# First-layer heads around the change of batch: GpSimd and the loads in the loop's order, and the batch-0 sums placed beside the row maxima

## What is computed

```python
q = jnp.einsum('bpd,hde->bphe', resid_pre, W_Q) + b_Q    # k, v alike
q = _apply_rotary(q, cos, sin)                           # k alike
scores = jnp.einsum('bqhd,bkhd->bhqk', q, k) / ATTN_SCALE
scores = jnp.where(causal[None, None], scores, 0)
max_v = jnp.max(jnp.abs(scores), axis=-1, keepdims=True)
sgn = jnp.sign(scores)
attn_w = sgn * jnp.exp(sgn * scores - max_v)
attn = attn_w / (jnp.sum(jnp.abs(attn_w), axis=-1, keepdims=True) + 1e-06)
z = jnp.einsum('bkhd,bhqk->bqhd', v, attn)
out = jnp.einsum('bqhd,hdm->bqm', z, W_O) + b_O
x = x + out
```

## Time and profile before

| | us |
|---|---|
| median of three executions | 864.09 |
| lowest and highest | 862.94, 867.29 |
| the profiled execution | 865.04 |
| its span, first to last instruction | 863.3 |
| TensorE busy | 828.1 |
| VectorE busy | 646.3 |
| ScalarE busy | 525.3 |
| GpSimd busy | 465.8 |
| mean granted share of TensorE's clock | 0.994 |

### The profile page before, as it was taken

One profiled execution on the slowest core, in us unless ns is written; L12 is line 12 of the kernel. 1 busy time (PEld: TensorE's weight loads), 2 busy tenths in 40 slices (PEclk: granted clock), 3 DMA queues, 4 the chain that ended last, 5 costly groups with the idle time before them and its releaser, 6 DMA issues.

```text
span 863.3 us, 14805 instructions
## 1 busy us (share of the span) xinstructions
PE 828.1 (96%) x4549; PEld 627.4 (73%) x4549; DVE 646.3 (75%) x1350; ACT 525.3 (61%) x1106; POOL 465.8 (54%) x399
## 2 busy tenths in 40 slices
PE   8899999999989999989998999999999999999997
PEld 6678788777878888766887887764444447888886
DVE  5898888999998888998376865868788634676553
ACT  3778788787867888863644533336576554454442
POOL 4565555666665556551666776623300426656774
PEclk9999999999999999999999999999999989999999
DMA  4222222322422223122665357412441132334442
GB/s 157 93 98 87 98 97 97 106 81 87 152 74 99 98 97 110 61 69 60 208 210 182 131 163 275 138 57 73 137 136 51 57 99 93 123 123 142 152 162 65
DMA packets 57426, 99.20 MB, mean 115 GB/s; under 512 B 8272, under 2 KB 19024, under 8 KB 57360
## 3 DMA queue, kind: packets, MB, share of 16 engines
q1 hardware_dynamic: 57360, 98.39, 34.3%
HBM read 71.88 MB, written 9.57 MB: 94 GB/s over the span
## 4 chain that ended last, share of the span: by engine, by line
PE 64%; issue 10%; POOL 10%; DVE 10%; ACT 4%; DMA 2%; SPq 0%; DVEq 0%; POOLq 0%; ACTq 0%
PE ps L974 10%; PE ps L951 10%; PE ps L960 9%; PE ps L319 6%; PE ps L382 5%; PE ps L330 4%; POOL q_sin L526 3%; PE ps L343 3%; PE ps L370 3%; PE ps L1642 2%; PE ps L1523 2%; PE ps L357 2%; PE ps L1612 2%; POOL wqk_lo L513 2%; DVE nm L1834 2%
## 5 line engine op out<-in xcount | busy, mean ns | idle before, releaser
L1098 POOL TENSOR_TENSOR ew_lo<-ew_raw,ew_hi 128x768 fp32r<-128x768 f32 x68 | 128.6, 1892 | 56.7 <-ACT ew_hi L1064 48.5
L1050 ACT ACTIVATE hid_hi<-guw 128x512 fp32r<-128x512 f32 x68 | 43.0, 632 | 156.2 <-POOL guw L1114 106.2
L1153 DVE TENSOR_TENSOR hid_lo<-guw,hid_hi 128x512 fp32r<-128x512 f32 x68 | 78.9, 1160 | 72.4 <-ACT hid_hi L1050 72.3
L1114 POOL TENSOR_TENSOR guw<-gu,cwb 128x512 f32<-128x512 f32 x61 | 80.4, 1318 | 92.4 <-issue 76.4
L526 POOL TENSOR_TENSOR q_sin<-q_sw,sin 128x512 f32<-128x512 f32 x64 | 83.5, 1312 | 51.7 <-DMA q_sw<-q_in 50.4
L1834 DVE TENSOR_REDUCE nm<-ps 128x1 f32<-128x512 f32 x128 | 81.4, 683 | 19.0 <-PE ps L1546 17.8
L1729 ACT ACTIVATE e<-ps 128x512 f32<-128x512 f32 x128 | 68.7, 602 | 35.6 <-PE ps L1642 35.3
L974 PE MATMUL ps<-ew_hi,hid_hi 128*128 128x256 f32 x272 | 78.3, 288 | 2.4 <-DVE hid_lo L1153 1.8
L505 DVE SCALAR_TENSOR_TENSOR w<-ex,rden,sgn 128x512 f32<-128x512 f32 (+3 forms) x128 | 79.0, 680 | 0.0
L433 ACT ACTIVATE ex<-sabs,nmax 128x512 f32<-128x512 f32 (+3 forms) x128 | 61.5, 551 | 28.1 <-DVE nmax L479 28.1
L974 PE MATMUL ps<-ew_lo,hid_hi 128*128 128x256 f32 x272 | 76.8, 282 | 0.0
(11 more groups left out here) (189 smaller groups left out, 2401.6 us busy)
## 6 DMA issues: line engine op xcount, KB each, us to landing
ew_raw<-in_ew SPq DMA_DIRECT2D x68, 384.0 KB, 3.3
q_sw<-q_in SPq DMA_DIRECT2D x128, 128.0 KB, 2.0
cwb<-cw_dram SPq DMA_DIRECT2D x61, 256.0 KB, 3.7
wqk_raw<-in_wqk SPq DMA_DIRECT2D x32, 256.0 KB, 2.6
wv_raw<-in_wv SPq DMA_DIRECT2D x32, 128.0 KB, 2.4
wo_raw<-in_wo SPq DMA_DIRECT2D x32, 128.0 KB, 2.2
qs<-stk_q SPq DMA_DIRECT2D x16, 256.0 KB, 3.5
ks<-stk_k SPq DMA_DIRECT2D x16, 256.0 KB, 4.1
```

The source lines that it names most:

```text
L1098: pool.tensor_tensor(ff[f].ew[1][:, i % EW_SLOTS, :], ew_raw[:, i % RAW_SLOTS, :], fp(ff[f].ew[0][:, i % EW_SLOTS, :]), ALU.subtract).then ...
L1114: pool.tensor_tensor(ff[f].guw[:, i % 2, :], ff[f].gu[:, i % 2, :], ff[f].cwb[:, r % CWB_SLOTS, :], ALU.mult).then_inc(sem("guw"), 1)
L1153: dve.tensor_tensor(ff[f].hid[1][:, i % 2, :], ff[f].guw[:, i % 2, :], fp(ff[f].hid[0][:, i % 2, :]), ALU.subtract).then_inc(sem("hid_lo"), 1)
```

## The change

`late(i)` is true in the loops and in steps 11 to 18, and takes the place of `not known(i)`. So steps 11 to 18 get the order that the loops have: on GpSimd `wqk_low` behind the causal selects and the wait for `den` ahead of `wo_lo`, on SyncE `wv_raw` ahead of `wo_raw` and `wqk_raw`. The two sums x+xn of steps 17 and 18 move from the end of the step to between the causal selects and `wqk_low`. The other steps that are written out, x+bo and `ffn_sp` stay where they are.

```diff
+        def late(i):
+            return not known(i) or H0 - 5 <= i <= H0 + 2
+
+        def x_take(pool, k):
+            pool.wait_ge(sem("x_bo0"), 2)
+            pool.wait_ge(sem("o_ev"), k + 1)
+            pool.tensor_tensor(x[:, 2 * k:2 * k + 2, :], x[:, 2 * k:2 * k + 2, :], xn[:, 2 * k:2 * k + 2, :],
+                               ALU.add).then_inc(sem("x_add"), 1)
+
         def a0_pool(pool, i):
-            if known(i):
+            if not late(i):
                 wqk_low(pool, i)
...
                     pool.affine_select(out=diag, in_=diag, compare_op=ALU.is_ge, fill=0.0, base=0,
                                        pattern=[[0, QT], [-1, P]], channel_multiplier=1).then_inc(sem("causal"), 1)
-            if not known(i):
+            if known(i) and H0 + 1 <= i <= H0 + 2:
+                x_take(pool, i - (H0 + 1))
+            if late(i):
                 wqk_low(pool, i)
...
                 wait(pool, "wo_hi", n + 1)
-                if not known(i):
+                if late(i):
                     wait(pool, "den", QT * (n + 2))
...
-            if not known(i):
+            if late(i):
                 load_wv(sp, i + 4)
...
                 sp.dma_start(wqk_raw[:, :, :, :], src).then_inc(sem("wqk_ld"), 16)
-                if known(i):
+                if not late(i):
                     load_wv(sp, n)
...
-            if i in (H0 + 1, H0 + 2):
-                k = i - (H0 + 1)
-                pool.wait_ge(sem("x_bo0"), 2)
-                pool.wait_ge(sem("o_ev"), k + 1)
-                pool.tensor_tensor(x[:, 2 * k:2 * k + 2, :], x[:, 2 * k:2 * k + 2, :], xn[:, 2 * k:2 * k + 2, :],
-                                   ALU.add).then_inc(sem("x_add"), 1)
```

## The result

The changed kernel takes 873.60 us (median of 4 runs, 872.72 to 876.26), the kernel before 864.23 us (4 runs, 862.94 to 867.29): a ratio of 1.0097, 95% interval 1.0055 to 1.0138. It is slower, by more than the 0.5% bound and outside the forecast range.

The account below looks back on a forecast made before the run. TensorE, busy 96% of the span, bounds the kernel. Gain 5.81 us, less 3.4 idle, 1.5 low clock and 0.66 for `x_take`, leaves 0.25: median 864.09 to 863.9 us, range 860.4 to 866.3 (the forecast's own 862.5 to 865.5).

Parts of the forecast that it names:

- What bounds the kernel: Whole kernel: TensorE is busy 96% of the span, so only changes to its idle time or clock count.
- the 5.81 us that the trace of before offered as gain: Steps 12, 14 and 18: 0.87, 0.99 and 3.95 us too long, all taken as recovered.
- "I take nothing for it" (x+bo on `w`): Steps 11 to 14: x+bo beside `w` costs nothing, though a neighbour lost 1.03 us; 0.87 if cover were gone.
- The burst in front of q_sw: Steps 16 to 18: expert loads issued about 4.3 us later delay step 17's q_sw; L319 of step 18 idles 3.4 us.
- `x_take` at 0.66 a step: Steps 17 and 18: x+xn ahead of `wqk_lo` costs 1.28 less 0.62 slack, 0.66 us idle; up to 1.1 if stretched.
- the lock of which the prediction spoke: VectorE and GpSimd's SBUF port pair: a VectorE instruction with two SBUF inputs holds it exclusively for its whole length.
- The 0.5 us a step: Steps 17 and 18: `wqk_lo` waits out the first L486, estimated at another 0.5 us a step.
- The den wait and `load_wv`: GpSimd's wait before `wo_lo` and SyncE's load issued ahead of `wo` and `wqk`: each costs nothing by itself.
- The clock: Step 18: 3.4 us of idle time brings the 1.2 GHz level, 1.5 us more; bounds nothing and 1.5.
- The sum: Steps 11 to 19: 5.56 us given back of 5.81 gained, 0.25 less; median 864.09 becomes 863.9.
- Rival B: L319 idle time behind steps 17 and 18 makes two low-clock stretches: 7.9 us back, 2.1 slower, 866.2; chance 0.11.

Follow-up runs that it names:

- Run 9: The kernel before, unaltered, for a second trace of steps 11 to 19; 867.83 against 866.24 us, ratio 1.0005.
- run 8: The kernel before with 17 more warm-up matmuls at its start, about 4.9 us; 878.81 against 872.38 us, ratio 1.0097.
- run 10: The changed kernel without x+bo of steps 11 to 14, so its output lacks that bias; 871.73 us against 866.24 for the kernel before, ratio 1.0056.
- run 1: The changed kernel, unaltered, for a second trace; 876.99 us against 869.85 for the kernel before, ratio 1.0109.
- run 12: The changed kernel, unaltered, in more executions beside as many of the kernel before; 872.98 against 866.10 us, ratio 1.0085.
- Run 3: The changed kernel with step 16's gw, ebias, lower4 and expert loads issued ahead of the wait for `wqk_lo`; 870.87 us against 869.85 for the kernel before, ratio 0.9997.
- run 4: The changed kernel with the x+xn sums back at the end of steps 17 and 18; 873.15 us against 869.85 for the kernel before, ratio 1.0032.
- run 7: The changed kernel with step 16's loads ahead and x+xn directly behind `wqk_lo`; 869.83 us against 872.38 for the kernel before, ratio 0.9979.
- run 5: The changed kernel with x+bo of steps 11 to 14 directly behind `wqk_lo`; 879.24 us against 872.38 for the kernel before, ratio 1.0081.
- run 2: The kernel before with only the x+xn sums of steps 17 and 18 moved between the causal selects and `wo_lo`; 869.40 against 869.85 us, ratio 0.9993.
- run 6: The changed kernel with step 16's loads ahead and both x+bo and x+xn directly behind `wqk_lo`; 870.79 us against 872.38 for the kernel before, ratio 0.9982.

## Why the prediction was wrong

**What bounds the kernel** held: TensorE's idle time and clock account for all of it. But the 5.81 us that the trace of before offered as gain were one draw. Run 9 has 6.2, shared otherwise among steps 12, 14 and 18, and run 8 3.1. A gain read from single steps of one execution was not tied to those steps.

**"I take nothing for it" (x+bo on `w`)** is the first step that failed. Its neighbour row, `w` at 2.96 with 1.03 lost, was the right price for one meeting; what I did not ask is what `w` would run into when 1.03 longer. The room to q_sin is 0.93 in the loop and 0.08 in step 14 of run 10, so `w` loses again (4.98 in step 14). Run 10 gives the price: 2.2 us in steps 12 and 14, where the sum had none and named 0.87 as the cost if its cover were gone. I looked at q_sin's idle 2.88 us only as room for GpSimd, not as the time until q_sin is itself in the way.

**The burst in front of q_sw** was the right mechanism and the right place: late `wqk` load, expert loads issued 4.2 us later (222.94 for 218.76), q_sw behind them, L319 of step 18 idle and released by `wqk_lo`. Its size was off: q_sin 9.96 us into the step, not 8.0; this is the second term that failed, 5.30 us of idle time and 5.55 of loss for 3.4. By the packets of the trace the expert loads themselves were nearly on time: the last of their packets (3072 bytes each) starts at 229.37, and the sum had them landed at 229.1. What was sized wrong is what comes behind them: the first pair of q_sw, for which the sum took 0.65 us, landed at 231.95, just before q_sin's start at 232.01. The second load of that pair took 7.0 us from its issue, and 6.9 and 7.1 in runs 1 and 12. I had priced it by the spacing of the expert loads; why it takes so much longer stays open. "DMA: Bandwidth & Descriptors", section "Queues, rings and completion order", of the Trainium skill has each engine take one ring's descriptors in order. The packets agree: those of q_sw (2048 bytes each) start from 228.87 on, so they overlap the last of the expert loads' by half a microsecond and stand behind all the others. The landings do not follow one another so strictly: the first q_sw landed at 230.0, 5.6 us after its issue, and the last expert load at 231.5, 7.6 after its own. Run 3 shows the price of standing behind: the same q_sw with the loads 4.3 us sooner let q_sin start about 3 us sooner in its step.

**`x_take` at 0.66 a step** held for step 19: 0.64 idle. In step 18, where the slack was already used, it costs its whole length and more: 1.72 and 1.81 by runs 4 and 7, where the sum had 1.28 in that chain. The 0.44 is `wqk_lo` beside L486, the upper end that I named and did not take. "SBUF — State Buffer", section "Who interferes with whom", of the Trainium skill says that a VectorE instruction with two SBUF inputs contends with GpSimd's reads and a tensor_reduce does not. The trace agrees on both (x+xn 1.27 beside the maxima; `wqk_lo` 1.72 and L486 1.61 where they meet). The lengths also fit the lock of which the prediction spoke, taken in turn from instruction to instruction: `wqk_lo` starts at 236.87 and is longer by 0.44, where the first instruction of L486 still runs until 237.47; the second starts at 237.40 and ends at 239.01, 0.42 behind the end of `wqk_lo` at 238.59. The 0.5 us a step that the prediction named as the estimate by that rule, and did not put into the sum, was near the mark.

**The den wait and `load_wv`** cost nothing, as said: both are in run 10, whose steps 11 to 15 lose nothing.

**The clock.** A dip came where forecast; 6.8 us at 0.50, and step 18 lost 3.04 - 0.64 = 2.4 us by it, not 1.5. The forecast took the length of the dip from the earlier trace rows, where the idle time was 2.19 and not 5.30. The idle time alone does not set that length either: dips of 6.8 us came with 5.30, 5.17 and 5.41 us of it (changed kernel, runs 1 and 12), but of 3.4 us with 5.23 (run 5), 4.54 (run 10) and 3.58 (run 4), and none with 2.16 (run 3), nearly the 2.19 that brought one before.

**The sum.** Forecast 5.81 - 5.56 = 0.25 gained in steps 11 to 19 (864.09 less 0.25 is 863.8, where the prediction has 863.9); measured 4.9 lost. Of these 5.2 (4.9 and 0.25), the steps 12 and 14 make 2.2 (0.51 + 1.66), the idle time of step 17 2.1 (5.55 for 3.4), the clock 0.9 (2.4 for 1.5). Rival B had the right side, and would have given 2.1 us slower. Its own mechanism, a second low-clock stretch from step 19's idle time, did not come; 0.64 was too little, as B itself had it. What lies above 5 us between the first two traces is the second layer's clock, of which no step of the prediction spoke; that it is so in the medians too is likely and not shown. The range of 860.4 to 866.3 had no allowance for it, though executions of the kernel before alone span 861.9 to 873.0 in run 12's set, and 860.0 to 881.9 over all sets.

## What to carry to other kernels

An order that costs nothing in a loop body costs nothing for the loop's own work alone: before adding an instruction to it, read the room from the end of the slowed neighbour to the next thing that it can meet, not to the next thing that waits for it, and read it in the step concerned (0.93 us in the loop, 0.08 in step 14). Before moving an instruction that frees a buffer, list everything queued behind the wait on that buffer, bulk loads above all, and issue them ahead of the wait (run 3: 3.1 us of idle time and a clock dip for two lines moved). A gain read from a few steps of one execution is first to be seen again in a second one.

## What the runs showed of the hardware

- VectorE's four `w` instructions lose 1.0 us to one 128x512 GpSimd instruction beside them and 2 to 3.4 us to two or three; GpSimd's own instructions stay at 1.28 or go to 1.44, 1.72 and 1.75. One instruction of L486 went from 0.55 to 1.61. The VectorE instruction that meets a GpSimd instruction ended 0.4 to 0.55 us behind it in two meetings (x+bo ends at 191.47 and the first instruction of `w` at 192.02; `wqk_lo` at 238.59 and L486 at 239.01).
- q_sin is started by a DMA and `w` by VectorE, each at its own pace, so their meeting is decided by less than 1 us. In the old order (both traces of the kernel before, runs 2 and 8) the step after one that lost 1 to 4 us loses nothing; in the new order it can (1.02 and then 1.88 in run 6). The same kernel lost 3.95 us in step 18 in one execution and in step 14 in another.
- In the second layer TensorE, 94 to 100% busy in the windows shown, is granted 0.50; over all traces such stretches last 3.4, 6.8, 10.2, 13.7 and 20.5 us, at places that differ between executions of one kernel. Each 0.001 of mean clock is about 0.6 us of this kernel.
- A 384 KB load took 4.1 to 5.1 us to land with the queue free behind it, and 4.6 to 7.6 with four 128 KB loads right behind (4.2 to 6.1 in run 1, 4.3 to 6.1 in run 12). The 128 KB loads, 2.0 us in the median, took 4.9 to 7.0 behind the three.
